# Bilinear sampling in a four-layer image kernel: corner products by one broadcast multiplication for three taps, additions over whole tiles, a convolution over two tiles, transposes of two taps

## What is computed

```python
def _bilinear_corner(x, yi, xi, wgt):
    valid = (yi >= 0) & (yi < H) & (xi >= 0) & (xi < W)
    v = jax.vmap(lambda im, yy, xx: im[:, yy, xx])(x, yc, xc)
    return v * (wgt * valid.astype(x.dtype))[:, None]
val = _bilinear_corner(x, y0, x0, (1 - ly) * (1 - lx)) + _bilinear_corner(x, y0, x0 + 1, (1 - ly) * lx) \
    + _bilinear_corner(x, y0 + 1, x0, ly * (1 - lx)) + _bilinear_corner(x, y0 + 1, x0 + 1, ly * lx)
mod = val * mask[:, None]
out = jnp.einsum('bckhw,ock->bohw', mod, weight.reshape(O, C, K)) + bias[None, :, None, None]
# batch norm with given statistics, relu
```

## Time and profile before

| | |
|---|---|
| runs | 4442.61, 4445.24, 4447.08 us |
| median | 4445.24 us |
| span of the profiled execution | 4440.6 us (its time outside the span isn't recorded; the median lies 4.6 us above the span) |
| granted TensorE clock, mean of the span | 0.913 |
| busy over the span | TensorE 3762 us (85%), VectorE 3350 (75%), GpSimd 2164 (49%), ScalarE 2024 (46%) |

### The profile page before, as it was taken

How to read it: one execution, slowest core, us unless ns; L and a number is a source line. 1 busy time by engine, 2 the same in 40 slices (tenths; PEclk the granted TensorE clock), 3 DMA queues, 4 the chain that set the end, 5 groups by cost and what they waited for, 6 DMA issues and landing times.

```text
span 4440.6 us, 76730 instructions
## 1 busy us (share of the span) xinstructions
PE 3762.3 (85%) x26409; PEld 2340.1 (53%) x26409; DVE 3349.5 (75%) x6753; ACT 2023.8 (46%) x4597; POOL 2164.1 (49%) x2457
## 2 busy tenths in 40 slices
PE   4999879879999968979999968987999977984454
PEld 2666624336777733435777743444777653433444
DVE  5666468659999857849999957848999967754666
ACT  2333342236666632235666743235666653222333
POOL 3222350038888641018887833006887835003775
PEclk9999989989999989989999989988999998986656
DMA  1000100055555400044555500025555520006776
GB/s 46 11 11 8 30 0 1 19 139 154 146 157 149 126 8 1 0 118 143 158 149 156 148 24 1 0 76 146 151 155 151 149 69 1 0 19 180 217 221 177
DMA packets 206461, 401.42 MB, mean 90 GB/s; under 512 B 23089, under 2 KB 121804, under 8 KB 204584
## 3 DMA queue, kind: packets, MB, share of 16 engines
q0 software_dynamic: 92160, 302.06, 23.8%
q1 hardware_dynamic: 113906, 94.92, 7.3%
q10 hardware_dynamic: 54, 0.01, 0.0%
HBM read 337.36 MB, written 59.53 MB: 89 GB/s over the span
## 4 chain that ended last, share of the span: by engine, by line
PE 45%; DVE 25%; issue 10%; POOL 10%; POOLq 4%; DVEq 3%; ACT 2%; DMA 1%; SPq 0%; ACTq 0%
PE bank L622 11%; DVE val L1168 8%; PE bank L494 8%; DVE mxc L1131 6%; DVE xl L1190 4%; POOL G L1515 3%; PE bank L475 3%; PE bank L476 3%; PE bank L477 3%; PE bank L478 3%; DVE val L1178 2%; PE bank L648 2%; POOLq L1490 2%; PE bank L664 2%; PE bank L443 2%
## 5 line engine op out<-in xcount | busy, mean ns | idle before, releaser
L796 ACT ACTIVATE pt<-bank 128x512 f32<-128x512 f32 x1024 | 608.8, 595 | 620.9 <-PE bank L478 619.0
L1525 POOL TENSOR_TENSOR xl<-pt 128x192 bf16<-128x192 f32 x1024 | 624.9, 611 | 532.0 <-PE bank L494 465.1
L1131 DVE TENSOR_REDUCE mxc<-bank 128x1 f32<-128x512 f32 x896 | 609.3, 681 | 159.5 <-PE bank L443 158.1
L1515 POOL DMA_INDIRECT G<-patch_table,idx x576 | 592.0, 1028 | 202.1 <-issue 115.3
L494 PEld LDWEIGHTS bank<-vt,pt 128*128 128x128 bf16 x8192 | 548.9, 98 | 239.0 <-issue 0.2
L494 PE MATMUL bank<-vt,pt 128*128 128x129 bf16 (+1 forms) x8192 | 632.3, 220 | 0.0
L1190 DVE TENSOR_TENSOR xl<-pt 128x320 bf16<-128x320 f32 x1024 | 541.6, 529 | 108.3 <-PE bank L494 89.3
L1297 DVE SCALAR_TENSOR_TENSOR G<-xn,vec,G 128x512 f32<-128x512 f32 x736 | 521.6, 748 | 47.2 <-issue 40.7
L1500 POOL TENSOR_TENSOR rs<-ve,mhalf 128x4 f32<-128x4 f32 x32 | 36.1, 1128 | 820.6 <-ACT ve L928 820.6
L494 PE MATMUL bank<-vt,xl 128*128 128x129 bf16 x4096 | 401.1, 221 | 5.3 <-DVE xl L1190 5.2
L475 PE MATMUL bank<-qh,regk 128*128 128x512 bf16 x1024 | 390.2, 381 | 3.1 <-ACT m L782 3.1
(11 more groups left out here) (243 smaller groups left out, 6804.1 us busy)
## 6 DMA issues: line engine op xcount, KB each, us to landing
patch_table<-valt SPq DMA_DIRECT2D x64, 512.0 KB, 7.0
G<-patch_table,idx POOLq DMA_INDIRECT x576
x_cur<-in_x SPq DMA_DIRECT2D x4, 2048.0 KB, 8.3
xl<-in_x SPq DMA_DIRECT2D x32, 256.0 KB
attn_out<-ob SPq DMA_DIRECT2D x32, 256.0 KB, 2.6
x_store<-x_cur SPq DMA_DIRECT2D x4, 2048.0 KB, 6.3
xr<-x_store SPq DMA_DIRECT2D x32, 256.0 KB
out<-fo SPq DMA_DIRECT2D x32, 256.0 KB
```

The lines of the kernel that those rows point to most:

```text
L796: A(pt[:, at % PT_RING, :], ST[at % ST_RING], ACT.Exp, scale=SCALE).then_inc(s["exp_done"], 1)
L1131: v.reduce_max(mxc[:, t, mc:mc + 1], MX[at % 2], AX.X).then_inc(s["mx_red"], 1)
L1515: g.indirect_dma_start(out=patches(j, k), out_offset=None, in_=table[:], in_offset=bass.IndirectOffsetOnAxis(ap=idx[:, j * K1 + k:j * K1 + ...
L1525: g.tensor_tensor(pl[:, at % PL_RING, 0:PL_POOL], pt[:, at % PT_RING, 0:PL_POOL], ph[:, at % PT_RING, 0:PL_POOL], ALU.subtract).then_inc(s ...
```

## The change

`SPT` becomes 6 and a new constant `TRR` = 5 counts the groups of transposes of a tile.

- VectorE, offsets 3 to 5: one TENSOR_TENSOR per part multiplies corners 2 and 3 of three taps (3 x 2 x 128 = 768 columns) in place in the patches by their weights, which are read with a step of 0 along the 128 channels (`corner_weights`). Offsets 6 to 8: three additions over all nine taps (1152 columns; for the slots in `regq` and `x_cur` 1024 and 128): corner 2 += corner 3, `val` += corner 2, `val` += corner 1. Before each a drain; after the last, a drain and `val_rdy`. The third multiplication is two instructions where the ninth tap lies apart.
- TensorE: transposes at offsets 10 to 14, two taps a group (the fifth has one), into columns 0 to 255. Convolution at offsets 15 and 16 of the odd tiles only, for two tiles at once: five taps' and four taps' matmuls of 256 columns, into columns 256 to 511.
- ScalarE: evacuations at 12 to 16, of 256 columns (the fifth 128); one result activation of 256 columns for two tiles, at offset 18 of the odd tile.
- The counts of the tail's waits follow; its work is the same.

```diff
-SPT = 7
+SPT = 6
+TRR = 5
@@ helpers
+        def held(j, first, stop):
+            slot = j % TB
+            if slot < 2:
+                return [(G[:, slot, first:stop, :], first, stop)]
+            most = (regq, x_cur)[slot - 2][:, 0:(K1 - 1) * PATCH].rearrange("p (k e) -> p k e", e=PATCH)
+            pieces = [(most[:, first:min(stop, K1 - 1), :], first, min(stop, K1 - 1))]
+            if stop == K1:
+                one = xlf[:, (slot - 2) * PATCH:(slot - 1) * PATCH].rearrange("p (k e) -> p k e", e=PATCH)
+                pieces.append((one, K1 - 1, K1))
+            return pieces
+
+        def corner_weights(j, first, stop, corner, end):
+            some = w4[:, j, :].rearrange("p (q k) -> p k q", k=K1)[:, first:stop, corner:end]
+            return bass.AP(some.tensor, some.offset, list(some.ap) + [[0, C]])
@@ dcn_transposes
-                    if j:
+                    if j and j % 2 == 0:
                         pe.wait_ge(s["res_rdy"], J)
-                else:
-                    pe.wait_ge(s["tr_ev"], 3 * J + r + 1)
-                for k in range(3):
-                    last = nc.tensor.transpose(TR[0][:, k * 128:(k + 1) * 128], val[:, j % 2, 3 * r + k, :],
+                if r or j % 2:
+                    pe.wait_ge(s["tr_ev"], TRR * J + r + 1)
+                for k in range(2 * r, min(2 * r + 2, K1)):
+                    last = nc.tensor.transpose(TR[0][:, k % 2 * 128:(k % 2 + 1) * 128], val[:, j % 2, k, :],
                                                ident[:])
@@ dcn_conv
-                piece = slice(j % TB * 128, (j % TB + 1) * 128)
+                piece = slice((j % TB - 1) * 128, (j % TB + 1) * 128)
...
-                for k in range(3 * r, 3 * r + 3):
-                    last = mm(TR[0][:, 384:512], dcnw_s[:, k, :], valt[:, k, piece],
+                for k in range(5 * r, min(5 * r + 5, K1)):
+                    last = mm(TR[0][:, 256:512], dcnw_s[:, k, :], valt[:, k, piece],
                               start=(k == 0), stop=(k == K1 - 1))
-                if r == 2:
-                    last.then_inc(s["conv_ps"], 1)
+                if r == 1:
+                    last.then_inc(s["conv_ps"], 2)
@@ TensorE's steps
-                        for part in range(3):
-                            j = tile_at(at, 11 + part)
+                        for part in range(TRR):
+                            j = tile_at(at, 10 + part)
                             if j is not None:
                                 dcn_transposes(n - 1, j, part)
-                            j = tile_at(at, 14 + part)
-                            if j is not None:
+                        for part in range(2):
+                            j = tile_at(at, 15 + part)
+                            if j is not None and j % 2:
                                 dcn_conv(n - 1, j, part)
@@ dcn_evacuate, ScalarE's steps
-                A(valt[:, 3 * r:3 * r + 3, piece], TR[0][:, 0:384].rearrange("p (k n) -> p k n", k=3), ACT.Copy)\
-                    .then_inc(s["tr_ev"], 1)
+                taps = min(2, K1 - 2 * r)
+                A(valt[:, 2 * r:2 * r + taps, piece],
+                  TR[0][:, 0:taps * 128].rearrange("p (k n) -> p k n", k=taps), ACT.Copy).then_inc(s["tr_ev"], 1)
...
-                        for part in range(3):
-                            j = tile_at(at, 13 + part)
+                        for part in range(TRR):
+                            j = tile_at(at, 12 + part)
                             if j is not None:
                                 dcn_evacuate(n - 1, j, part)
@@ dcn_result
-                A(fo[:, j % TB * 128:(j % TB + 1) * 128], TR[0][:, 384:512], ACT.Relu, bias=bn[:, 3:4],
-                  scale=bn[:, 2:3]).then_inc(s["res_rdy"], 1)
+                A(fo[:, (j % TB - 1) * 128:(j % TB + 1) * 128], TR[0][:, 256:512], ACT.Relu, bias=bn[:, 3:4],
+                  scale=bn[:, 2:3]).then_inc(s["res_rdy"], 2)
@@ interpolate
-                if r < SPT - 1:
-                    for o in range(3 * r, 3 * r + 3):
-                        corner, k = 2 + o // K1, o % K1
-                        if corner > 2 and k == 0:
-                            dve.drain()
-                        src = patches(j, k)[:, corner * C:(corner + 1) * C]
-                        dst = val[:, j % 2, k, :]
-                        v.scalar_tensor_tensor(dst, src, w4[:, j, corner * K1 + k:corner * K1 + k + 1], dst,
-                                               ALU.mult, ALU.add)
-                else:
+                if r < 3:
+                    for patch, first, stop in held(j, 3 * r, 3 * r + 3):
+                        far = patch[:, :, 2 * C:4 * C].rearrange("p k (q c) -> p k q c", c=C)
+                        v.tensor_tensor(far, far, corner_weights(j, first, stop, 2, 4), ALU.mult)
+                    return
+                if r == SPT - 1:
                     dve.wait_ge(s["c1_rdy"], m * T + j + 1)
-                    dve.drain()
...
+                dve.drain()
+                for patch, first, stop in held(j, 0, K1):
+                    q = (2, 2, 1)[r - 3] * C
+                    if r == 3:
+                        into, other = patch[:, :, 2 * C:3 * C], patch[:, :, 3 * C:4 * C]
+                    else:
+                        into, other = dst[:, first:stop, :], patch[:, :, q:q + C]
+                    v.tensor_tensor(into, into, other, ALU.add)
+                if r == SPT - 1:
                     dve.drain()
                     dve.sem_inc(s["val_rdy"], 1)
```

More of the change, by code:

```diff
@@ L381, in _ @@
             mm = nc.tensor.matmul
-            pe.sem_inc(s["tr_ps"], 4)
+            pe.sem_inc(s["tr_ps"], TRR + 1)
             for name in ("mo", "xt_ps", "ot_ps"):
@@ L727, in tail_transposes @@
                 for r in range(3):
-                    pe.wait_ge(s["tr_ev"], 3 * (TAIL + j) + r - 2 + 1)
+                    pe.wait_ge(s["tr_ev"], TRR * TAIL + 3 * j + r - 2 + 1)
                     for k in range(3):
@@ L736, in tail_conv @@
                 q, t = j // TB, j % TB
-                pe.wait_ge(s["tr_ev"], 3 * (TAIL + j + 1) + 1)
+                pe.wait_ge(s["tr_ev"], TRR * TAIL + 3 * (j + 1) + 1)
                 if t == 0 and q >= 2:
@@ L808, in first_corner @@
                 if part == 0:
-                    act.wait_ge(s["tr_ps"], 3 * (m * T + j) + 1)
+                    act.wait_ge(s["tr_ps"], TRR * (m * T + j) + 1)
                     act.wait_ge(gathered(j), landed(m, j))
@@ L868, in attention @@
                     if dcn:
-                        for part in range(3):
-                            j = tile_at(at, 13 + part)
+                        for part in range(TRR):
+                            j = tile_at(at, 12 + part)
                             if j is not None:
                                 dcn_evacuate(n - 1, j, part)
+                        for part in range(3):
                             j = tile_at(at, 1 + part)
@@ L985, in tail_corner @@
                 act.wait_ge(gathered(j), landed(N - 1, j))
-                act.wait_ge(s["tr_ps"], 3 * (TAIL + j) + 1)
+                act.wait_ge(s["tr_ps"], TRR * TAIL + 3 * j + TRR - 2)
                 for k in range(K1):
@@ L996, in tail_evacuate @@
                 for r in range(3):
-                    act.wait_ge(s["tr_ps"], 3 * (TAIL + j) + r + 1 + 4)
+                    act.wait_ge(s["tr_ps"], TRR * TAIL + 3 * j + r + 1 + TRR + 1)
                     A(valt[:, 3 * r:3 * r + 3, t * 128:(t + 1) * 128],
@@ L1157, in interpolate @@
             def interpolate(m, j, r):
+                dst = val[:, j % 2]
                 if r == 0:
                     dve.wait_ge(s["c0_rdy"], m * T + j + 1)
-                if r < SPT - 1:
-                    for o in range(3 * r, 3 * r + 3):
-                        corner, k = 2 + o // K1, o % K1
-                        if corner > 2 and k == 0:
-                            dve.drain()
-                        src = patches(j, k)[:, corner * C:(corner + 1) * C]
-                        dst = val[:, j % 2, k, :]
-                        v.scalar_tensor_tensor(dst, src, w4[:, j, corner * K1 + k:corner * K1 + k + 1], dst,
-                                               ALU.mult, ALU.add)
-                else:
-                    dve.wait_ge(s["c1_rdy"], m * T + j + 1)
-                    dve.drain()
-                    slot = j % TB
-                    joint = K1 if slot < 2 else K1 - 1
-                    held = G[:, slot] if slot < 2 else (regq, x_cur)[slot - 2][:, 0:joint * PATCH]\
-                        .rearrange("p (k e) -> p k e", e=PATCH)
-                    dst = val[:, j % 2, 0:joint, :]
-                    v.tensor_tensor(dst, dst, held[:, :, C:2 * C], ALU.add)
-                    if joint < K1:
-                        dst = val[:, j % 2, joint, :]
-                        v.tensor_tensor(dst, dst, patches(j, joint)[:, C:2 * C], ALU.add)
+                if r < 3:
[4 more added lines that the diff above has]
+                if r == SPT - 1:
```

(3 more changed lines are left out.)

6 lines of the change are left out of this document (3 added, 3 removed).

## The result

The change made the kernel slower: 4566.82 us (median of 4 runs, 4564.22 to 4571.58) against 4445.24 beside it, a ratio of 1.0276 with a 95% interval of 1.0263 to 1.0288. The prediction was 4505 us, slower by 1.3%; the direction came, with twice the size, and the time lies 7 us above the top of the range, 4560. The profiled execution has a span of 4569.8 us, 129.2 more than before.

A forecast was written before the change was run, and what follows sets the result against it. VectorE was taken as first bound, TensorE close behind; GpSimd's +49 us against 39 of slack left 10, plus 10 for coupling: 20 us a stage, x 3 = 60, 4445 + 60 = 4505 us. Range 4400 to 4560.

The forecast's parts named there:

- GpSimd's slack: In attention stages with sampling, GpSimd's waiting for data, without issue gaps, was its spare time: 39 us in 521.
- GpSimd's subtraction: GpSimd's low-value subtraction, held up by VectorE: 0.18 us per added addition, 0.07 per multiplication, less 8 us coming back.
- Its own sign of failure: GpSimd still waiting 20 us or more for data and VectorE idling more would mean TensorE binds and the time fell.
- TensorE's and ScalarE's part: Wider convolution passes (0.215 us each) and five transpose groups: TensorE 2 us a stage less, ScalarE's extra evacuations hidden.
- The gathers: GpSimd's gathers held up by long VectorE instructions: 0.39 us per addition, less per multiplication by a squared ratio, 0.37.
- The bound of +75 - 39 = +36: Upper limit a stage: GpSimd loses 75 us if arrivals are evenly spread, less 39 us of slack.
- The 10 us for coupling: Added to each stage because two tightly coupled engines at the limit leave some 10 us of waits.
- Predicted -8 us a stage: VectorE in each sampling stage: 16 us more interpolation work, less 24 us of contention relief (none to 48).
- The first: Rival: VectorE's relief decides because GpSimd's loss stays under 39 us; -15 us a stage, 4400 us; chance 0.24.
- The second: Rival: gathers are not held up, GpSimd's remaining 10 us fit its slack, VectorE's -8 shows; 4421 us; chance 0.04.
- The third: Rival: GpSimd's added waits just fill its slack, within 0.2%; 4445 us; chance 0.09.
- The fourth: Rival: the multiplications' step-0 operand costs twice a column, +77 us a stage on VectorE; about 4670 us; chance 0.03.

The follow-up runs named there:

- e10: Kernel before with TensorE's and ScalarE's part of the change, old interpolation in seven parts, everything behind the tile one step later; 4439.49 us, ratio 0.9988.
- e11: Changed kernel with transposes, evacuations, convolution, result and residual one step later; 4562.91 us, ratio 1.0265.
- e8: Changed kernel with GpSimd issuing five of a tile's nine gathers, the other four taps by plain loads on ScalarE's queue; 4546.29 us, ratio 1.0230.
- e12: Changed kernel with both the one-step shift of e11 and the five gathers of e8; 4498.35 us, ratio 1.0124.
- e2: Changed kernel with the old interpolation put back, packed into six parts; 4481.48 us, ratio 1.0080.
- e9: Kernel before with GpSimd issuing five of a tile's nine gathers, the other four taps by plain loads on ScalarE's queue; 4417.80 us, ratio 0.9934.
- e3: Changed kernel with its three additions written as SCALAR_TENSOR_TENSOR times 1.0, multiplications still TENSOR_TENSOR; 4574.37 us, ratio 1.0281.
- e13: e11 with all interpolation in TENSOR_TENSOR of 384 columns, six multiplications and nine additions a tile; 4545.27 us, ratio 1.0224.
- e1: Kernel before with VectorE's part of the change alone, TensorE and ScalarE as before; 4581.11 us, ratio 1.0300.

## Why the prediction was right in sign and short by half

**The bound and the floor: right.** The prediction read GpSimd's slack as 39 us, and said that data waits near zero would show it used up. Counted to the end of the last gather they fell from 43 us to 5. It said that TensorE would then wait for GpSimd's subtraction; it waits 45 us. Its own sign of failure (GpSimd waits 20 us or more, VectorE idles) did not come.

**TensorE's and ScalarE's part: right.** Ten convolution passes of 256 columns last 2.16 us in a piece of the chain, 0.216 each (0.215 predicted), and e10 shows the whole part at -0.12%.

```profile
1084.99 2.16 PE bank L536 x10
```

What it didn't see is that the odd tile now comes late to its first transpose: "the distance from `val_rdy` to the first transpose is two steps, as before" holds for the steps' numbers, not for the work, for the three additions now lie in the last parts of the tile. (That they are what makes it late is argued; that the tile is late is shown by the waits for `val_rdy`, and by the shift that removes them.) It is hidden behind GpSimd in the changed kernel (e11: 1 to 4 us a stage) but worth 12 to 17 once GpSimd is out of the way (599 to 603 in e8, 587 in e12).

**The gathers: right in sum, in part by luck.** Predicted +39 us of excess a stage, measured +43 (31.4 to 74.2). The price of an addition came out the same: 44 gathers in the 96 additions lost 37.8 us, 0.39 for each addition. But it is a product whose factors both moved: before, 22 gathers met 32 additions and lost 0.57 us each; now 44 met 96 and lost 0.86 each. Fewer meetings and dearer ones cancelled, which the prediction gave no reason for. A multiplication cost 0.25 (59 gathers, 24.1 us) where the squared ratio gave 0.145, and the rest of the gathers lost 6 us less. Minimum durations were as sized: additions 1357 ns, multiplications 941 with their tail.

```profile
L1187 DVE TENSOR_TENSOR G<-G,w x48: 941/1057/1274, 1005.0 to 1545.0; 128x768 f32<-128x768 f32 x48
L1198 DVE TENSOR_TENSOR val<-val,G x32: 1357/1487/1733, 1014.8 to 1552.6; 128x1152 f32<-128x1152 f32 x32
```

**GpSimd's subtraction: the term that failed.** Predicted +10 us (0.18 for each of 64 more additions, 0.07 for each of 96 multiplications, less 8), measured +37.5 (31.1 to 68.6). The 0.18 came from 8 subtractions that started in 32 additions. With three additions in neighbouring steps 51 started in 96, twice as often, and lost 39.2 us: 0.41 each, just the value for evenly spread arrivals which the prediction named as its bound and didn't take. Multiplications cost 0.20 each (37 hits, 19.1 us) instead of 0.07. The cost of one meeting hardly moved (5.8/8 = 0.73 us before, 39.2/51 = 0.77 after). I had taken the rate of meeting, 8 in 32, for a property of the instruction, but it belongs to the place where the instruction stands: the same 32 old additions were met 13 times in e2 and 15 times in e10. What came back from the old chains, 8 us in the sum, was 15 (all other subtractions lost 25 us before and 10 after), so the additions and multiplications alone were 34 us short.

**The sum then closes.** Gathers +43 and subtraction +37 are +80 us (VectorE's effect on GpSimd's busy time in the stages, 452 to 532, is the same 80). Less the 38 of data wait that were used up (43 to 5) that is 42, and the stage grew by 44. The bound of +75 - 39 = +36 was the right form and 8 us low. The 10 us for coupling are hardly seen (44 - 42 = 2), and the 2 are themselves what two changes leave that the sum has no term for: GpSimd's issue gaps grew by 9 us a stage (40 to 49), and its waits behind the last gather and its shortest gaps shrank by 6. In the prediction's terms, of the 24 us a stage that it was short, the subtraction is 27, the gathers are 4 and the slack is 1, less 8 of the 10 that it had set for coupling.

**VectorE: rightly off the path, wrongly summed.** Predicted -8 us a stage; its busy time rose by 11. The interpolation's lines sum to 261.9 us before and 260.6 after, -1; if the added work was the 16 us of the sum, the relief from contention was about as large. The +27 us that the Trainium skill's instruction cost (VectorE: DVE Perf Modes, the section on the trn2 errata) would have given aren't borne out by these lines. But VectorE's own subtraction rose from 545 to 581 ns, +9 us, which I had not looked at: it is the contention in the other direction. With GpSimd out of the way and the transposes shifted, the change still costs 26 us a stage (e12 against e9) where I had a small gain; that VectorE's part is what costs them is argued, from e10, where TensorE's part was worth nothing beside the full load of gathers. So the loss has three bounds one behind another: GpSimd held up (616), the odd tile late for transposes that stand too near to it (599 to 603), and VectorE with what it meets (587). Freeing the first alone brought no gain over the kernel before.

**The rivals.** The first (VectorE's relief decides) needed GpSimd's loss under 39 us; it was 80 by the instructions' excess. The second, the rule of the Trainium skill (SBUF — State Buffer, section "Who interferes with whom") that `tensor_tensor` doesn't stall descriptor generation, does not hold for these gathers, which read their indices from SBUF: gathers inside TENSOR_TENSOR lost 0.86 us each in the additions (37.8/44), and in e3 as much (37.9/44) in SCALAR_TENSOR_TENSOR. No run has another kind of transfer issued by GpSimd. The third, a balance within 0.2%, needed GpSimd's loss to stop at its slack. The fourth, a broadcast operand that costs twice, did not come: 768 columns took 0.94 us at the least, where two times 1.047 ns a column would be 1.6.

## What to carry to other kernels

Before replacing many short VectorE instructions with few long ones, look at what GpSimd does beside them: here its gathers and its subtraction, once begun beside a long one with two SBUF inputs, finished only some 0.8 and 0.36 us after that one had ended, and if GpSimd has less slack than that costs, the change loses whatever VectorE gains. Look at the other direction too, since the held-up work runs into VectorE's next instruction. Take the price of one meeting from the trace, but work out the number of meetings anew for the place where the new instructions go, with even spread as the upper value. And when an experiment frees the bound and the time stays, list the waits again: here each freed bound showed the next one.

## What the runs showed of the hardware

- A gather issued while a VectorE instruction of 768 columns or more with two SBUF inputs ran ended about 0.83 us after that instruction (multiplications and additions of the changed kernel); so did one begun beside SCALAR_TENSOR_TENSOR once this was 1024 or 1152 columns long (e3). Beside the old instructions of 128 columns 86 gathers lost 2.7 us in all, beside e13's multiplications of at most 384 columns 62 lost 9.3.
- GpSimd's own TENSOR_TENSOR is held up in the same way, by 0.77 us (39.2/51) in an addition and 0.52 (19.1/37) in a multiplication.
- The hold works both ways. VectorE's own subtraction, unchanged in size, took 568 to 588 ns on average where the interpolation was in long instructions (after, e1, e3, e8, e11, e12), 519 to 545 with the old one (before, e2, e9, e10), and 547 with pieces of 384 columns (e13). Beside nothing of GpSimd's it took 0.48 us in all of these; in the changed kernel 58 began while GpSimd's subtraction ran and lost 14.8 us, 40 lost 8.7 in the kernel before.
- A float32 convolution pass of 256 columns took 0.216 us where one of 128 took 0.112: joining two tiles saved 3 to 4% of it.
- A weight operand with step 0 cost a multiplication nothing that shows: 0.94 us for 768 columns, tail included.
